# A windowed-attention stack: the local attention output transposed in 32x32 blocks by VectorE, in place of TensorE transposes and ScalarE copies

## The chip, the cores and the metric

The kernel runs on one core of a Trainium2 chip. The metric is the device time of one execution in microseconds; here the median of 3 runs. The core has TensorE (PE, matmuls, writes PSUM only), VectorE (DVE), ScalarE (ACT), GpSimd (POOL) and SyncE (SP, which issues the DMAs). Each engine works through its own queue of instructions in order and is synchronised with the others by semaphores.

## The reference

Input is x of 8 x 512 x 128 (f32). With xn = layer norm of x, the output is x + global_attention(xn) + local_stack(xn). The local stack has 6 layers. Each layer, with `shift` moving the second half of the channels down by one token:

```
x = attn_layer(shift(x)) + x ;  x = ffn_layer(shift(x)) + x
attn_layer: q, k, v = split(x @ Wqkv) in 16 heads of 64; q, k l2-normalised, scaled, rotated
            windows of 32 tokens; each window attends to itself and the window before it, masked
            out = softmax(q k^T * 8) v, per head;   return out (tokens x 1024) @ Wo
ffn_layer:  layer norm, W1 (a and gate), a * gelu(gate), W2
```

The change concerns the step between softmax(...) v and the product with Wo: `out` has tokens in partitions where it is computed, and Wo's product needs channels in partitions.

## The kernel before

Layer norm and the global attention come first (the first 690 us or so). Then `windowed_stack` runs 48 units, one for each layer and batch element (512 tokens, four tiles of 128). xT holds x with channels in partitions.

A unit is cut into stages, named by a kind and a tile number: `q0` (projection), `square_q0`, `rotate_q0`, `norms0`, `root0`, `scale_q0` (normalising and rotating), `qT0`, `kT0` (PE transposes), `s0` (scores, DVE subtracts the maximum), `exp0`, `r0` (transposes of the probabilities), `va0`, `vb0` (probabilities times v, heads 0-7 and 8-15), `o0` (transposes of the output), `wo`, `mean`, `var`, `z`, `h0` to `h2`, `y` (feed-forward).

The order of the stages on each engine is written out by hand in PE_ORDER, DVE_ORDER, ACT_ORDER, POOL_ORDER and SP_ORDER. A name with `-` belongs to the previous unit, so two units overlap. Nothing is planned at run time: an engine takes the stages in that order, and each stage waits for its inputs (`x_filled`, `x_read`, events such as `rooted`). PSUM is four slots of two banks; SLOTS_OF names the stages that share a slot, and a stage on PE also waits until the stage before it in its slot has been read.

Around the change, for each tile:
- PE `va`, `vb` (`products`): 32x32 blocks of probabilities times v. One column of v is 1, so that column 64 of each 65 is the sum. Window order in PSUM is that of WINDOWS = (1, 3, 0, 2).
- DVE `va`, `vb` (L836, L837): reciprocal of the sums, product into `o` (tokens in partitions, 1024 elements), a link semaphore between the two.
- PE `o` (L967 with `ident,o`): eight 128x128 transposes into PSUM. ACT `o` (L926): one copy into `oT` [128, 8, 512], windows put back in order. It waits for the previous unit's `wo`.
- PE `wo` (L1037): eight matmuls of 512 columns over the chunks of oT, after the copy of tile 3. DVE `residual` adds x into x1; ACT `shift` (L938, L872, L873) makes xs2 from it; PE `mean`, DVE `center` (L846) and so on.

At a layer's end SP waits for DVE's `y` and loads the feed-forward weights, w_o among them, in five DMAs (`load_ff`); PE, DVE and ACT wait for all five. w_qkv is loaded in three parts as their last use passes. POOL does `add` (cosq + sinq, L734) and the steps of the square root (L726). The v halves are shifted by a window into `vb` with DMAs.

Of the kernel before, what the change touches and what calls it, by code (L numbers as in the profile page):

```python
# [12 lines left out]
P = 128  # L13
D = 128
# [17 lines left out]
NJ = 3  # L32
# [167 lines left out]
def global_attention(nc, io, res, xT, ident):  # L200
# [6 lines left out]
    with ExitStack() as ctx:  # L207
# [227 lines left out]
        def _(pe):  # L435
# [75 lines left out]
PE_ORDER = stages(  # L511
    "o0- r1- s2- q0 kT3- va1- k0 vb1- qT3- r2- o1- s3- va2- vb2- q1 r3- k1 o2- qT0 va3- vb3- kT0 k2 o3- s0 wo- q2 "
    "v0 mean- qT1 r0 var- v1 kT1 k3 va0 s1 h0- h1- h2- vb0 q3 v2 qT2 y- kT2 v3 ")
DVE_ORDER = stages(
# [3 lines left out]
ACT_ORDER = stages(  # L518
    "o0- r1- v3- square_q0 kT3- square_k0 exp2- qT3- r2- o1- exp3- square_q1 r3- o2- qT0 square_k1 kT0 o3- "
    "square_k2 exp0 shift- square_q2 v0 square- qT1 r0 root- kT1 v1 gate0- square_k3 gate1- gate2- exp1 square_q3 "  # L520
# [12 lines left out]


FILLS = {"q": (TPB, "dve"), "k": (TPB, "dve"), "v": (TPB, "act"), "qT": (TPB, "act"), "kT": (TPB, "act"),
         "s": (TPB, "dve"), "r": (TPB, "act"), "va": (TPB, "dve"), "vb": (TPB, "dve"), "o": (TPB, "act"),
         "wo": (1, "dve"), "mean": (1, "dve"), "var": (1, "act"), "h": (NJ, "dve"), "y": (1, "dve")}
# [3 lines left out]
          "q_scaled": ("dve", TPB), "k_scaled": ("dve", TPB), "probs": ("act", TPB),  # L541
          "xs2_ready": ("act", 1), "centered_sq": ("act", 1), "z_ready": ("dve", 1), "gates": ("act", NJ)}
EVENTS.update({kind + "_filled": ("pe", n) for kind, (n, _) in FILLS.items()})
# [4 lines left out]
VTILES = 3  # L548
WINDOWS = (1, 3, 0, 2)


def windowed_stack(nc, io, xT, ident):
# [5 lines left out]
    with ExitStack() as ctx:  # L558
# [37 lines left out]
        o = sb("o", [P, 2, 4, 2, DH])  # L596
        oT = sb("oT", [P, QCH, SEQ])
        x1 = sb("x1", [P, SEQ])
# [21 lines left out]
        def wait_tile(eng, name, unit, t, back=1):  # L620

            wait(eng, name, unit + (t - back) // TPB, (t - back) % TPB)
# [39 lines left out]
        def _(sp):  # L662
# [4 lines left out]
            def load_ff(l):  # L667
                sp.dma_start(w_o[:, :, :], io["w_o"][l].rearrange("(c p) n -> p c n", p=P)).then_inc(S["w_ff"], 16)
                sp.dma_start(w_1[:, :, :, :].rearrange("p a j n -> p (a j n)"), io["w_1"][l]).then_inc(S["w_ff"], 16)
                sp.dma_start(w_2[:, :, :], io["w_2"][l].rearrange("(j p) n -> p j n", p=JW)).then_inc(S["w_ff"], 16)  # L670
                sp.dma_start(b_1[:, :, :].rearrange("p a j -> p (a j)"), io["b_1"][l]).then_inc(S["w_ff"], 16)
                sp.dma_start(vec[:, :], io["vec"][l]).then_inc(S["w_ff"], 16)
# [66 lines left out]
        def _(dve):  # L739
# [49 lines left out]
            def stage(kind, n, unit, batch, before, starts):  # L789
# [40 lines left out]
                elif kind in ("va", "vb"):  # L830
                    a = ("va", "vb").index(kind)
                    wait(dve, kind + "_filled", unit, n)

                    wait_tile(dve, "o_filled", unit, n)
                    ps = slot(kind, n)[:, :, 0:4 * VA].rearrange("p r (w d) -> p r w d", d=VA)
                    link(nc.vector.reciprocal(rden[:, a], ps[:, :, :, DH]), kind, 0)  # L836
                    nc.vector.tensor_tensor(o[:, a].rearrange("p w r d -> p r w d"), ps[:, :, :, 0:DH],  # L837
                                            rden[:, a, :, :, None].broadcast_to([P, 2, 4, DH]), ALU.mult).then_inc(S[kind + "_read"], 1)
                elif kind == "residual":
                    wait(dve, "wo_filled", unit)  # L840
# [25 lines left out]
        def _(act):  # L866
# [12 lines left out]
            def stage(kind, n, unit, batch, before, starts):  # L879
# [7 lines left out]
                elif kind == "v":  # L887

                    old, unit_of = (0, unit) if n == VTILES else ((TPB - 1 if n == 0 else n), unit - 1)
                    wait(act, "vb_filled", unit_of, old)  # L890
                    wait_vb(act, unit_of, old)
# [25 lines left out]
                elif kind == "r":  # L917
                    wait(act, "r_filled", unit, n)

                    wait_tile(act, "vb_filled", unit, n)  # L920
                    nc.scalar.copy(probT[:, :, :], flat("r", n).rearrange("p (c n) -> p c n", n=P)).then_inc(S["r_read"], 1)
                elif kind == "o":
                    wait(act, "o_filled", unit, n)

                    wait(act, "wo_filled", unit - 1)
                    nc.scalar.copy(oT[:, :, n * P:(n + 1) * P].rearrange("p c (w n) -> p w c n", n=WIN),  # L926
                                   flat("o", n).rearrange("p (w c n) -> p w c n", w=4, n=WIN)).then_inc(S["o_read"], 1)
                elif kind == "next":
# [27 lines left out]
        def _(pe):  # L956
# [6 lines left out]

            def transposes(kind, n, src, place=lambda c: c):
                for c in range(8):
                    k = place(c)
                    last = nc.tensor.transpose(flat(kind, n)[:, k * P:(k + 1) * P], src[:, c * P:(c + 1) * P], ident[:, :])  # L967
                return last
# [17 lines left out]
            def products(kind, t):  # L986
                a = ("va", "vb").index(kind)
                for r in range(2):
                    for n, v in enumerate((va, vb)):
                        for g in range(4):  # L990

                            last = nc.tensor.matmul(  # L992
                                slot(kind, t)[32 * g:32 * g + 32, r, 2 * n * VA:2 * (n + 1) * VA],
                                probT[:, 4 * a + 2 * r + n, 32 * g:32 * g + 32],
                                v[:, t % VTILES, :, 2 * (4 * a + g) + r, :],
                                start=True, stop=True, skip_group_check=True)
                return last

            def stage(kind, n, unit, batch, before, starts):
# [22 lines left out]
                elif kind in ("va", "vb"):  # L1022
                    if kind == "va":
                        wait(pe, "r_read", unit, n)
                        wait_vb(pe, unit, n)
                    passed(pe)
                    last = products(kind, n)
                elif kind == "o":
                    wait(pe, "va_read", unit, n)
                    wait(pe, "vb_read", unit, n)  # L1030

                    last = transposes(kind, n, o[:, :, :, :, :].rearrange("p a w r d -> p (a w r d)"),
                                      lambda c: 2 * WINDOWS[c % 4] + c // 4)
                elif kind == "wo":
                    wait(pe, "o_read", unit, TPB - 1)
                    for c in range(QCH):
                        last = nc.tensor.matmul(slot("wo")[:, 0, :], w_o[:, c, :], oT[:, c, :], start=c == 0, stop=c == QCH - 1)  # L1037
                elif kind == "mean":
# [126 lines left out]
```

## Time and profile before

| | before |
|---|---|
| median of 3 runs (lowest, highest) | 4495.01 us (4487.22, 4496.09) |
| span of the profiled execution | 4494.6 us (no other time of it is given) |
| PE busy | 4032.1 us, 90% |
| DVE busy | 3861.7 us, 86% |
| ACT busy | 2887.1 us, 64% |
| POOL busy | 1723.6 us, 38% |
| DMA, q1 | 122.47 MB, 11.4% of 16 engines |
| granted TensorE clock, mean of the span | 0.976 of full speed |

Busy time counts an engine's instructions, not register, branch, semaphore or DMA-issuing ones. Matmuls are pipelined, so a group's duration overlaps with the next group's, and the step from one start to the next is what a group costs. DVE instructions overlap slightly too. An idle time in front of an instruction is put down to what released it. PEld is PE's loading of weights, which runs beside the matmuls.

### The profile page before, as it was taken

To read this page: it belongs to the slowest core of one execution; us is meant where nothing else is said; L and a number is where in the kernel's file an instruction comes from. 1 tells how busy PE (TensorE), PEld (TensorE's weight loads), DVE (VectorE), ACT (ScalarE), POOL (GpSimd) and SP (SyncE) were. 2 spreads that over 40 slices of the span, in tenths; PEclk is the share of its full clock that TensorE was granted. 3 is DMA by queue.
4 is the path that set the end of the run, shared out by engine and by line. 5 is a ranking of instruction groups with operands and counts; after the bars stand their busy time and mean duration, and the time that the engine had idled before them with its cause. 6 is when DMAs were issued, how large, how long until landed. Compare 5 with 4: busy or idle time off the path is not lost. (4 is left out here: it accounts for less than half of the span.)

```text
span 4494.6 us, 104653 instructions
## 1 busy us (share of the span) xinstructions
PE 4032.1 (90%) x38560; PEld 2304.6 (51%) x38560; DVE 3861.7 (86%) x5604; ACT 2887.1 (64%) x3434; POOL 1723.6 (38%) x3226
## 2 busy tenths in 40 slices
PE   5888885999998999989999989999899999899996
PEld 2333333555555555555555555555455555555554
DVE  6888877898988999978999879898889998798985
ACT  3666663676766666666767666666666666576764
POOL 2222213444443434434444434444343434344441
PEclk8999997999999999999999999999999999999998
DMA  0000002010111111120101111110211111110102
GB/s 25 1 1 1 1 1 71 22 32 21 32 33 37 27 26 27 26 53 19 34 19 31 38 36 27 23 30 21 52 23 29 24 26 43 32 32 19 35 18 56
DMA packets 65070, 123.99 MB, mean 28 GB/s; under 512 B 15684, under 2 KB 37576, under 8 KB 64968
## 3 DMA queue, kind: packets, MB, share of 16 engines
q1 hardware_dynamic: 64968, 122.47, 11.4%
q8 instruction: 84, 1.38, 0.1%
q14 instruction: 18, 0.15, 0.0%
HBM read 21.99 MB, written 4.19 MB: 6 GB/s over the span
## 5 line engine op out<-in xcount | busy, mean ns | idle before, releaser
L734 POOL TENSOR_TENSOR cosq<-cosq,sinq 128x1024 f32<-128x1024 f32 x384 | 970.9, 2528 | 1665.5 <-DVE sinq L784 1665.5
L1010 PE MATMUL slot<-w_qkv,xs 128*128 128x512 f32 x2304 | 1096.5, 606 | 54.3 <-ACT xs L873 26.6
L819 DVE TENSOR_TENSOR qk<-cosq,ry 128x1024 f32<-128x1024 f32 x384 | 587.7, 1550 | 93.2 <-POOL ry L726 48.3
L1010 PEld LDWEIGHTS slot<-w_qkv,xs 128*128 128x128 f32 x2304 | 406.4, 191 | 474.4 <-issue 379.7
L784 DVE TENSOR_TENSOR sinq<-slot,table 128x512 f32<-128x512 f32 x768 | 490.6, 680 | 0.0
L781 DVE TENSOR_TENSOR cosq<-slot,table 128x1024 f32<-128x1024 f32 x384 | 467.9, 1218 | 18.8 <-ACT sq L885 6.8
L910 ACT COPY kT<-slot 64x1024 f32<-64x1024 f32 x384 | 386.6, 1007 | 120.6 <-PE slot L967 116.8
L916 ACT ACTIVATE prob<-prob 128x1024 f32<-128x1024 f32 x192 | 203.0, 1057 | 388.8 <-DVE prob L828 387.1
L803 DVE TENSOR_REDUCE ss<-sq 128x32 f32<-128x2048 f32 x192 | 437.3, 2277 | 11.3 <-ACT sq L885 11.3
L967 PEld LDWEIGHTS slot<-ident,qk 128*128 128x128 f32 x3072 | 345.1, 142 | 180.1 <-issue 92.8
L885 ACT ACTIVATE sq<-slot 128x1024 f32<-128x1024 f32 x384 | 392.5, 1022 | 66.9 <-PE slot L1010 65.6
L967 PE MATMUL slot<-ident,qk 128*128 128x128 f32 x3072 | 409.8, 277 | 16.1 <-DVE o L837 7.9
L979 PE MATMUL slot<-kT,qT 128*32 128x128 f32 x12288 | 417.2, 276 | 7.5 <-issue 7.5
L979 PEld LDWEIGHTS slot<-kT,qT 128*32 128x32 f32 x12288 | 313.0, 110 | 106.6 <-issue 106.4
L372 DVE TENSOR_REDUCE at_rowmax<-at_slot 128x1 f32<-128x512 f32 x512 | 317.1, 684 | 50.6 <-PE at_slot L459 50.3
L1037 PE MATMUL slot<-oT,w_o 128*128 128x512 f32 x768 | 342.4, 599 | 1.2 <-ACT oT L926 1.2
L992 PE MATMUL slot<-va,probT 128*32 128x130 f32 x6144 | 318.0, 277 | 22.9 <-DVE sinq L784 22.9
L425 ACT ACTIVATE at_probs<-at_slot 128x1024 f32<-128x1024 f32 x256 | 245.8, 1027 | 130.2 <-PE at_slot L473 130.1
L1047 PE MATMUL slot<-xs,w 128*114 128x512 f32 x576 | 261.0, 603 | 70.3 <-DVE xs L854 70.3
L992 PE MATMUL slot<-vb,probT 128*32 128x130 f32 x6144 | 312.7, 273 | 0.0
L827 DVE TENSOR_REDUCE smax<-slot 128x16 f32<-128x1024 f32 x192 | 233.5, 1216 | 67.1 <-PE slot L979 67.1
L726 POOL TENSOR_TENSOR rt<-ry 128x32 f32<-128x32 f32 x576 | 137.3, 238 | 377.1 <-DVE ry L810 346.9
(130 smaller groups left out, 6568.9 us busy)
## 6 DMA issues: line engine op xcount, KB each, us to landing
vb<-va SPq DMA_DIRECT2D x720, 130.0 KB, 2.3
w_qkv<-in_w_qkv SPq DMA_DIRECT2D x18, 512.0 KB, 4.5
w_o<-in_w_o SPq DMA_DIRECT2D x6, 512.0 KB
w<-in_w SPq DMA_DIRECT2D x6, 342.0 KB
res<-in_x SPq DMA_DIRECT2D x4, 512.0 KB, 6.2
kept<-res SPq DMA_DIRECT2D x1, 2048.0 KB, 8.7
out<-fin_res SPq DMA_DIRECT2D x8, 256.0 KB, 2.4
w<-in_w SPq DMA_DIRECT2D x6, 171.0 KB
```

The costliest lines, as they stand in the source:

```text
L734: nc.gpsimd.tensor_tensor(cosq[:, side], cosq[:, side], sinq[:, side], ALU.add).then_inc(S["qk"[side] + "_added"], 1)
L781: nc.vector.tensor_tensor(cosq[:, side].rearrange("p h a d -> p h (a d)"), ps.rearrange("p h a d -> p h (a d)"), cos[:, None, :].broadcast ...
L784: last = nc.vector.tensor_tensor(sinq[:, side, :, half, :], ps[:, :, 1 - half, :], sin[:, None, half * H:half * H + H].broadcast_to([P, HE ...
L803: nc.vector.reduce_sum(ss[:, :], sq[:, :, :, :].rearrange("p a h d -> p (a h) d"), AX.X).then_inc(S["sumsq"], 1)
L819: nc.vector.tensor_tensor(qk[:, side], cosq[:, side].rearrange("p h a d -> p h (a d)"), ry[:, side * HEADS:(side + 1) * HEADS, None].broad ...
L885: nc.scalar.activation(sq[:, "qk".index(name)].rearrange("p h d -> p (h d)"), flat(name, n), ACT.Square).then_inc(S[name + "_squared"], 1)
L910: nc.scalar.copy(own[rows, :, r, WIN:WIN + P], ps[rows])
L967: last = nc.tensor.transpose(flat(kind, n)[:, k * P:(k + 1) * P], src[:, c * P:(c + 1) * P], ident[:, :])
L979: last = nc.tensor.matmul(slot("s", t)[32 * g:32 * g + 32, a, :].rearrange("p (r k) -> p r k", r=2)[:, :, n * DH:(n + 1) * DH], qT[:, c, t ...
L992: last = nc.tensor.matmul(slot(kind, t)[32 * g:32 * g + 32, r, 2 * n * VA:2 * (n + 1) * VA], probT[:, 4 * a + 2 * r + n, 32 * g:32 * g + 3 ...
L1010: last = nc.tensor.matmul(slot(kind, n)[:, i, :], xs[:, n * P:(n + 1) * P], w_qkv[:, "qkv".index(kind), i * SEQ:(i + 1) * SEQ], start=True ...
L1037: last = nc.tensor.matmul(slot("wo")[:, 0, :], w_o[:, c, :], oT[:, c, :], start=c == 0, stop=c == QCH - 1)
```

## The change

The `o` stages leave PE and ACT. DVE gets a stage `turn` per tile, behind `vb`: one transpose instruction that turns every 32x32 block of `o` (128x1024) into `oT`. It doesn't move blocks across partitions, so a partition of oT holds the 32 channels of one half of a head in one of four groups of heads; w_o's rows are reordered on the host to match, which makes its load one contiguous row per partition. `products` writes the windows in natural order at a pitch of 66. `wo` reads its 512 columns in runs of 32.

```diff
 PE_ORDER = stages(
-    "o0- r1- s2- q0 kT3- va1- k0 vb1- qT3- r2- o1- s3- va2- vb2- q1 r3- k1 o2- qT0 va3- vb3- kT0 k2 o3- s0 wo- q2 "
+    "r1- s2- q0 kT3- va1- k0 vb1- qT3- r2- s3- va2- vb2- q1 r3- k1 qT0 va3- vb3- kT0 k2 s0 wo- q2 "
     "v0 mean- qT1 r0 var- v1 kT1 k3 va0 s1 h0- h1- h2- vb0 q3 v2 qT2 y- kT2 v3 ")
 DVE_ORDER = stages(
-    "scale_k3- scale_q3- s2- rotate_q0 va1- vb1- norms0 rotate_k0 s3- va2- vb2- scale_q0 rotate_q1 scale_k0 va3- "
-    "vb3- norms1 rotate_k1 s0 scale_q1 scale_k1 rotate_k2 residual- center- rotate_q2 norms2 z- va0 s1 scale_q2 hid0- "
-    "scale_k2 hid1- vb0 hid2- rotate_k3 norms3 rotate_q3 y- ")
+    "scale_k3- scale_q3- s2- rotate_q0 va1- vb1- turn1- norms0 rotate_k0 s3- va2- vb2- turn2- scale_q0 rotate_q1 scale_k0 va3- "
+    "vb3- turn3- norms1 rotate_k1 s0 scale_q1 scale_k1 rotate_k2 residual- center- rotate_q2 norms2 z- va0 s1 scale_q2 hid0- "
+    "scale_k2 hid1- vb0 turn0 hid2- rotate_k3 norms3 rotate_q3 y- ")
 ACT_ORDER = stages(
-    "o0- r1- v3- square_q0 kT3- square_k0 exp2- qT3- r2- o1- exp3- square_q1 r3- o2- qT0 square_k1 kT0 o3- "
+    "r1- v3- square_q0 kT3- square_k0 exp2- qT3- r2- exp3- square_q1 r3- qT0 square_k1 kT0 "
     "square_k2 exp0 shift- square_q2 v0 square- qT1 r0 root- kT1 v1 gate0- square_k3 gate1- gate2- exp1 square_q3 "
...
     "k0 kT0 s0 q1 kT1 s1 q2 qT2 kT2 s2 va3 h2",
-    "va0 o0 va1 o1 va2 o2 q3 vb3 o3 wo mean var h1",
+    "va0 va1 va2 q3 vb3 wo mean var h1",
     "q0 v0 r0 k1 r1 vb1 r2 vb2 k3 y",)
...
 FILLS = {"q": (TPB, "dve"), "k": (TPB, "dve"), "v": (TPB, "act"), "qT": (TPB, "act"), "kT": (TPB, "act"),
-         "s": (TPB, "dve"), "r": (TPB, "act"), "va": (TPB, "dve"), "vb": (TPB, "dve"), "o": (TPB, "act"),
+         "s": (TPB, "dve"), "r": (TPB, "act"), "va": (TPB, "dve"), "vb": (TPB, "dve"),
          "wo": (1, "dve"), "mean": (1, "dve"), "var": (1, "act"), "h": (NJ, "dve"), "y": (1, "dve")}
...
           "q_scaled": ("dve", TPB), "k_scaled": ("dve", TPB), "probs": ("act", TPB),
-          "xs2_ready": ("act", 1), "centered_sq": ("act", 1), "z_ready": ("dve", 1), "gates": ("act", NJ)}
+          "xs2_ready": ("act", 1), "centered_sq": ("act", 1), "z_ready": ("dve", 1), "gates": ("act", NJ),
+          "turned": ("dve", TPB)}
 EVENTS.update({kind + "_filled": ("pe", n) for kind, (n, _) in FILLS.items()})
...
 WINDOWS = (1, 3, 0, 2)
+PITCH = VA + 1
...
         o = sb("o", [P, 2, 4, 2, DH])
-        oT = sb("oT", [P, QCH, SEQ])
+        oT = sb("oT", [P, TPB, 2, 4, 2, 2, 32])
         x1 = sb("x1", [P, SEQ])
...
             def load_ff(l):
-                sp.dma_start(w_o[:, :, :], io["w_o"][l].rearrange("(c p) n -> p c n", p=P)).then_inc(S["w_ff"], 16)
+                sp.dma_start(w_o[:, :, :].rearrange("p c n -> p (c n)"), io["w_o"][l]).then_inc(S["w_ff"], 16)
                 sp.dma_start(w_1[:, :, :, :].rearrange("p a j n -> p (a j n)"), io["w_1"][l]).then_inc(S["w_ff"], 16)
...
-                    wait_tile(dve, "o_filled", unit, n)
-                    ps = slot(kind, n)[:, :, 0:4 * VA].rearrange("p r (w d) -> p r w d", d=VA)
+                    wait_tile(dve, "turned", unit, n)
+                    ps = slot(kind, n)[:, :, 0:4 * PITCH].rearrange("p r (w d) -> p r w d", d=PITCH)
                     link(nc.vector.reciprocal(rden[:, a], ps[:, :, :, DH]), kind, 0)
...
                                             rden[:, a, :, :, None].broadcast_to([P, 2, 4, DH]), ALU.mult).then_inc(S[kind + "_read"], 1)
+                elif kind == "turn":
+
+                    wait(dve, "vb_read", unit, n)
+                    wait(dve, "wo_filled", unit - 1)
+                    nc.vector.transpose(oT[:, n, :, :, :, :, :].rearrange("p a w r e t -> p (a w r e t)"),
+                                        o[:, :, :, :, :].rearrange("p a w r d -> p (a w r d)")).then_inc(S["turned"], 1)
                 elif kind == "residual":
...
                     old, unit_of = (0, unit) if n == VTILES else ((TPB - 1 if n == 0 else n), unit - 1)
-                    wait(act, "vb_filled", unit_of, old)
+                    for name in ("va", "vb"):
+                        wait(act, name + "_filled", unit_of, old)
                     wait_vb(act, unit_of, old)
...
-                    wait_tile(act, "vb_filled", unit, n)
+                    for name in ("va", "vb"):
+                        wait_tile(act, name + "_filled", unit, n)
                     nc.scalar.copy(probT[:, :, :], flat("r", n).rearrange("p (c n) -> p c n", n=P)).then_inc(S["r_read"], 1)
-                elif kind == "o":
-                    wait(act, "o_filled", unit, n)
-
-                    wait(act, "wo_filled", unit - 1)
-                    nc.scalar.copy(oT[:, :, n * P:(n + 1) * P].rearrange("p c (w n) -> p w c n", n=WIN),
-                                   flat("o", n).rearrange("p (w c n) -> p w c n", w=4, n=WIN)).then_inc(S["o_read"], 1)
                 elif kind == "next":
...
-            def transposes(kind, n, src, place=lambda c: c):
+            def transposes(kind, n, src):
                 for c in range(8):
-                    k = place(c)
-                    last = nc.tensor.transpose(flat(kind, n)[:, k * P:(k + 1) * P], src[:, c * P:(c + 1) * P], ident[:, :])
+                    last = nc.tensor.transpose(flat(kind, n)[:, c * P:(c + 1) * P], src[:, c * P:(c + 1) * P], ident[:, :])
                 return last
...
                             last = nc.tensor.matmul(
-                                slot(kind, t)[32 * g:32 * g + 32, r, 2 * n * VA:2 * (n + 1) * VA],
+                                slot(kind, t)[32 * g:32 * g + 32, r, 0:4 * PITCH].rearrange("p (w d) -> p w d", d=PITCH)[
+                                    :, (1 - n)::2, 0:VA],
                                 probT[:, 4 * a + 2 * r + n, 32 * g:32 * g + 32],
...
                 elif kind in ("va", "vb"):
-                    if kind == "va":
-                        wait(pe, "r_read", unit, n)
-                        wait_vb(pe, unit, n)
+                    wait(pe, "r_read", unit, n)
+                    wait_vb(pe, unit, n)
                     passed(pe)
                     last = products(kind, n)
-                elif kind == "o":
-                    wait(pe, "va_read", unit, n)
-                    wait(pe, "vb_read", unit, n)
-
-                    last = transposes(kind, n, o[:, :, :, :, :].rearrange("p a w r d -> p (a w r d)"),
-                                      lambda c: 2 * WINDOWS[c % 4] + c // 4)
                 elif kind == "wo":
-                    wait(pe, "o_read", unit, TPB - 1)
+                    wait(pe, "turned", unit, TPB - 1)
                     for c in range(QCH):
-                        last = nc.tensor.matmul(slot("wo")[:, 0, :], w_o[:, c, :], oT[:, c, :], start=c == 0, stop=c == QCH - 1)
+                        a, r, half = c // 4, c // 2 % 2, c % 2
+                        last = nc.tensor.matmul(slot("wo")[:, 0, :], w_o[:, c, :], oT[:, :, a, :, r, half, :],
+                                                start=c == 0, stop=c == QCH - 1)
                 elif kind == "mean":
...
         "qk_scale": np.broadcast_to(scales, (DEPTH, P, 2 * DH)),
-        "w_o": f["ffn_Wo"],
+        "w_o": f["ffn_Wo"].reshape(DEPTH, 2, 4, 4, 32, D).transpose(0, 2, 4, 1, 3, 5).reshape(DEPTH, P, QCH * D),
         "w_1": w1.reshape(DEPTH, D, 2 * NJ * JW),
```

## Rows read from the trace of the kernel before

**Rows 1.** The page, part 1: busy time and share of the span of each engine.
```profile
PE 4032.1 (90%) x38560; PEld 2304.6 (51%) x38560; DVE 3861.7 (86%) x5604; ACT 2887.1 (64%) x3434; POOL 1723.6 (38%) x3226
```

**Rows 2.** ACT's instruction at L938, by tile: count, shortest/median/longest ns, first and last start.
```profile
L938 ACT ACTIVATE xs<-zero x48: 199/199/201, 810.3 to 4448.0; 64x1 f32<-64x1 f32 x48
```

**Rows 3.** Stretches: length, then busy us (count) of PE, PEld, DVE, ACT, POOL; clock; DMA.
```profile
2677.66:2753.68 76.02, 72.04 (x735) 43.06 (x734) 69.00 (x85) 51.47 (x62) 32.02 (x56) 1.00 0.12 27
2591.05:2677.66 86.61, 74.35 (x735) 45.05 (x734) 67.19 (x85) 51.45 (x62) 31.99 (x56) 0.94 0.15 36
```

**Rows 4.** DVE's waits, 2677.66 to 2753.68 us: total, times, longest us.
```profile
DVE xc L846 <- PE slot L1040: 2.8, 1, 2.8
DVE qk L819 <- POOL ry L726: 1.1, 1, 1.1
DVE rden L836 <- PE slot L992: 0.8, 2, 0.5
DVE smax L827 <- PE slot L979: 0.5, 1, 0.5
DVE sqc L850 <- ACT sqc L945: 0.3, 1, 0.3
DVE ss L803 <- ACT sq L885: 0.2, 1, 0.2
```

**Rows 5.** DVE and POOL in order of time: start, duration us, instruction, [idle before it].
```profile
2711.43 4.35 DVE L819 TENSOR_TENSOR qk<-cosq,ry 128x1024 f32<-128x1024 f32 x2 [1.13 <-POOL ry L726]
...
2721.80 0.21 DVE L836 RECIPROCAL rden<-slot 128x8 f32<-128x8 f32 x1 [0.46 <-PE slot L992]
...
2722.04 0.69 DVE L837 TENSOR_TENSOR o<-slot,rden 128x512 f32<-128x512 f32 x1
...
2722.65 2.27 DVE L803 TENSOR_REDUCE ss<-sq 128x32 f32<-128x2048 f32 x1
...
2745.85 2.36 POOL L734 TENSOR_TENSOR cosq<-cosq,sinq 128x1024 f32<-128x1024 f32 x1
...
2747.24 3.19 DVE L819 TENSOR_TENSOR qk<-cosq,ry 128x1024 f32<-128x1024 f32 x2
```

**Rows 6.** PE in order of time, same unit.
```profile
2709.91 1.04 PE L967 MATMUL slot<-ident,o 128*128 128x128 f32 x8
...
2710.79 1.04 PE L967 MATMUL slot<-ident,prob 128*128 128x128 f32 x8
...
2712.98 0.39 PE L972 MATMUL slot<-mask,ident 128*128 128x512 bf16 x1
...
2720.65 0.43 PE L992 MATMUL slot<-va,probT 128*32 128x130 f32 x8 [0.43 <-DVE sinq L784]
...
2731.61 1.06 PE L967 MATMUL slot<-ident,prob 128*128 128x128 f32 x8 [0.60 <-ACT prob L916]
```

**Rows 7.** DVE instructions by line: count, shortest/median/longest ns.
```profile
L388 DVE STREAM_TRANSPOSE at_oT<-at_po x32: 716/717/718, 84.9 to 673.5; 128x512 f32<-128x512 f32 x32
L803 DVE TENSOR_REDUCE ss<-sq x192: 2272/2275/2287, 710.6 to 4406.2; 128x32 f32<-128x2048 f32 x192
L819 DVE TENSOR_TENSOR qk<-cosq,ry x384: 1209/1215/3319, 717.6 to 4416.5; 128x1024 f32<-128x1024 f32 x192
```

**Rows 8.** In order of time: a weight change (DVE and PE), and the trace's end.
```profile
2551.17 1.22 DVE L827 TENSOR_REDUCE smax<-slot 128x16 f32<-128x1024 f32 x1 [2.97 <-PE slot L979]
...
2632.15 1.94 PE L967 MATMUL slot<-ident,o 128*128 128x128 f32 x8 [8.69 <-DMA vec<-in_vec]
...
2633.89 1.92 PE L967 MATMUL slot<-ident,prob 128*128 128x128 f32 x8
...
2637.57 0.39 PE L972 MATMUL slot<-mask,ident 128*128 128x512 bf16 x1
...
2639.13 1.22 DVE L827 TENSOR_REDUCE smax<-slot 128x16 f32<-128x1024 f32 x1 [4.74 <-PE slot L979]
...
4449.61 2.05 PE L1040 MATMUL slot<-xs,ones 128*128 128x512 f32 x2 [2.36 <-ACT xs L873]
```

## The prediction

> **What bounds the kernel now.** I read the page's totals first. TensorE (PE) is busy for 90% of the span and VectorE (DVE) for 86% [rows 1], so either could be the limit. The work repeats, so the next view is one steady repetition. A program in the windowed stack handles 48 units (6 layers x 8 batch elements); ACT's small write at L938 occurs once per unit. It has 48 starts, 810.3 to 4448.0 us [rows 2]: 47 intervals, of which the last has no next unit behind it. I reckon with the 46 others. A middle interval takes 76.02 us, and in it PE is busy 72.04 and DVE 69.00 us [rows 3]. The longer interval in the same group is one where the weights change.
>
> Busy time doesn't say who waits for whom. DVE's own waits in that interval add up to 2.8+1.1+0.8+0.5+0.3+0.2 = 5.7 us [rows 4], so 70.3 of its 76.0 us is occupied. The question is which of these waits could absorb new DVE work. I followed each in the timeline:
> - 2.8 us (xc at L846): DVE writes x1, ACT shifts it, PE averages it, DVE goes on. No other DVE work stands between the two in DVE's order. It can't shrink because DVE gets busier.
> - 1.1 us (qk at L819, stages `scale_k3-`): DVE has seeded the square root, Pool (POOL) does 12 small steps, DVE fills the time with `rotate_q3` and `y-`. It starts from DVE's seeds, so it moves with DVE.
> - 0.8 us (rden) is two waits. The 0.46 before `vb1-` [rows 5]: PE had itself waited 0.43 for DVE's sinq [rows 6], because the PSUM slot of `vb1` holds `q0`. It hangs on DVE. The other 0.39, before `va3-`, ends with PE products that follow a long PE run. It is real slack.
> - 0.5 us (smax, `s0`) ends with PE scores.
> - 0.3 us (sqc) is at the end of an ACT run that begins with DVE's x1; 0.2 us (ss, `norms3`) ends with ACT's square. Only the last is slack for work put just ahead of it.
>
> So the loop that sets 76 us already runs mainly through DVE, and most of DVE's idle time is the latency of loops that DVE itself starts. PE's 4 us of idle time are mostly waits for them.
>
> **What the change removes.** Per unit, 4 groups of 8 PE transposes (`o`), each with one ACT copy of 128x1024 into oT. A group's duration is 1.04 us but the next group starts 0.88 us after it [rows 6], so PE is relieved of 4 x 0.88 = 3.5 us and ACT of four copies. Almost nothing of this is on the loop above. PE waits longer instead. Where it does reach the end is at the weight changes (below).
>
> **What it adds.** Per unit, 4 DVE transposes of 128x1024 f32, SBUF to SBUF, each behind a wait for the multiply just before it. The trace has no such instruction, but it has the same operation on 512 elements from PSUM: 716/717/718 ns [rows 7]. For the other 512 elements I use the slope between the shortest L819 (1209 ns, 1024 elements) and L803 (2275 ns, 2048 elements): 1.04 ns each, 533 ns. That gives 1.25 us. Bounds: 0.72 us if it handles two elements at a time, and 3.3 us, the longest L819, if it were held up each time by POOL [rows 7]. L803, which like the new instruction has one SBUF input, is within 2272 and 2287 ns in all 192 cases while L819 with two spreads from 1209 to 3319. I therefore take 1.25.
>
> Around it: without a wait the next DVE instruction starts 0.61 us after a 0.69 us multiply starts, and with one 0.03 us after the previous end (0.24 against 0.21) [rows 5]. The new wait therefore costs 0.69+0.03-0.61 = 0.11 us, and the following instruction recovers 0.08. One `turn` is 0.11+1.25-0.08 = 1.28 us, four are 5.12 us.
>
> The Trainium skill (VectorE: DVE Perf Modes, The three transpose paths) lists 390 ns for a TensorE transpose of 128x128 bf16 against 311 ns on VectorE. By this the exchange of 32 such tiles would look like a gain, 12.5 us of TensorE for 10.0 of VectorE per unit (an estimate from that page). The rows differ on both sides: a TensorE one costs the stream 0.11 us here, and the f32 DVE row makes eight tiles 1.25 us.
>
> **Where each turn falls.**
> - `turn0`, between `vb0` and `hid2`: all gates' inputs but the last were released earlier, so ACT's path is unchanged. `norms3` had 0.20 us of waiting. DVE is late by 1.28-0.20 = 1.08 us, and so are the seeds, POOL's root and `scale_k3-`. PE's `y-` waits for `hid2`, but comes over 1 us behind it.
> - `turn1`, before `norms0`: 1.28 in full. Behind it on DVE stand norms0, rotate_k0 and s3; ACT's exponential, then PE's `r3-`, wait for s3.
> - `turn2`, before `scale_q0`: 1.28, less the 0.39 of `va3-`, since PE comes there earlier by the missing `o2`. `qT0` on PE waits some 0.3 us for scale_q0, which leaves va3 still in time.
> - `turn3`, before `norms1`: 1.28 in full. The 0.5 us at `s0` vanish but win nothing: `scale_q1`, `scale_k1` take 3.19 us instead of 2.3 because POOL's cosq addition runs until 2748.21 [rows 5], and that addition follows norms1 through POOL. This wait is only renamed.
> - The mean on PE comes 0.1 us earlier, as PE is now idle before it.
>
> Sum: 5.12-0.20-0.39-0.10 = 4.43 us per interval, 76.0 becomes 80.4. DVE would be busy 69.0+5.0 = 74.0 us of it, PE 72.0-3.5 = 68.5.
>
> **Weight changes.** Each of 5 stretches over two intervals. In the first DVE waits 2.97 us for PE's scores behind a stall of PE's issue; there the 1.08 us of turn0 is absorbed, and the missing `o0` (0.88) brings the scores forward: -1.96. In the second, everything stands until the feed-forward weights are there, then PE does o0, r1, s2 while DVE waits 4.74 us; o0's step is 1.74 us there, at the lower clock: -1.74 [rows 8]. Together -3.7 each, -18.5 in all. The w_o load in 4 KB rows instead of 512 B may bring up to 2 us per change; it is one of five loads awaited together, so I take 0.
>
> **Costed at nothing.** The products write rows at a pitch of 66 and windows in another order: same columns, same DVE reads (bounds +-0.1 us per unit). wo's input is read in runs of 32: PE has about 1 us to spare before the mean. The extra `va_filled` waits on ACT concern earlier PE work. Ahead of the first and behind the last of the 46 intervals, turns partly fall into waits and the o3-copy latency before the last wo goes: 0, +-5 us.
>
> Forecast: 4494.6 + 46 x 4.43 - 18.5 = 4679.9, say 4680 us. The page gives the profiled execution's span, 4494.6, and no other time of it; the median of the timed runs is 4495.0, so I add nothing.
>
> **Rivals.**
> 1. *Faster: the idle time on DVE absorbs the turns.* If every wait in rows 4 could shrink, the interval would be DVE's occupied time, 70.3+5.1 = 75.4, -0.6 us: 4494.6-28-18.5 = 4448 us. It decides if PE, 90% busy, is the true bound and DVE's waits are all its doing. For: PE's higher busy share. Against: PE's recorded waits end with DVE or with ACT work that DVE released, and 2.8+1.1 us come from chains that DVE starts. Break-even needs 4.4 us more slack than I found. 7%.
> 2. *The transposes run at twice the rate* (0.72 us, lower bound): a turn costs 0.75, the interval +3.00-0.69 = +2.3: 4494.6+106-17 = 4584 us. Against: the 512-element row has the plain rate, if from PSUM. 8%. The Trainium skill (Vector Engine (DVE) Microarchitecture Reference, Performance modes) names copy, cast, tensor_scalar and tensor_tensor as what has faster modes enabled, and the transpose isn't among them; no run shows it yet for SBUF.
> 3. *The PE clock falls.* PE's idle gaps grow: before `vb1` 0.43+0.88+1.08 = 2.4 us, before `r3` 0.60+0.88+1.28 = 2.8 us [rows 6]. At the end of the trace PE takes 2.05 us for the mean's two matmuls after a gap of 2.36 us [rows 8], which is slow for 512 columns: the same engine does eight of 128 in 1.04 [rows 6]. From the two levels at a weight change: o0, r1 and half of s2 took 5.4 us at 1.2 GHz, then 2.4 [rows 8], against 3.1 in mid-layer [rows 6], +2.3. Once per unit and unhidden: 46 x 2.3 = +106, 4786 us; half hidden about 4735. Against: those gaps stand alone between dense stretches, and the steady interval grants 1.00 [rows 3]. 12%.
> 4. *Nothing to be told* (within 0.2%, about what this kernel's measurement can resolve, 9 us): some mix of 1 and 2. 3%.
>
> **Chances.** My forecast 70%, its own range 4650 to 4710 (turn 1.2 to 1.4 us, loads, pitch). Rivals 7, 8, 12 and 3%. Slower by over 0.2%: 0.90; within: 0.03; faster: 0.07. The 8-in-10 range, reaching toward rivals 2 and 3: 4600 to 4740.
>
> **What would show it.** A mid-layer interval of 80.4 us; DVE STREAM_TRANSPOSE at 1.25 us x192; xc's wait still 2.7 to 2.8 and the POOL wait still 1.1; rden's waits near 0.46 and smax's near 0 in an interval; PE waiting over 2 us at `vb1` and `r3`; granted clock still 1.00; DVE's wait at a weight change 1.7 us shorter. I am wrong if DVE's waits in an interval sum to under 2 us (rival 1), if the transposes take 0.7 us, or if the clock of a mid-layer interval is under 0.95.

## The result and the profile after

The changed kernel takes 4684.4 us (median of 4 runs, 4681.55 to 4686.1), the kernel before in the same series 4495.6 (median of 4): a ratio of 1.042, 95% interval 1.0405 to 1.0435. It is slower by 189 us. The forecast was 4680. The profiled execution took 4685.08 us with a span of 4683.3.

Part 1 of the page of the changed kernel, against [rows 1]:

```profile
PE 3833.7 (82%) x36769; PEld 2136.3 (46%) x37024; DVE 4114.1 (88%) x5796; ACT 2708.4 (58%) x3242; POOL 1722.9 (37%) x3226
```

PE lost 198 us of busy time and gave all of it back as idle time. DVE gained 252 us, more than the kernel became longer. These totals alone don't say which engine sets the time: they would fit any case in which one engine gets heavier and another lighter.

The instruction that starts a unit's feed-forward part, now at L942, by tile, and one mid-layer interval and one at a weight change (columns as in [rows 3]: length, busy us of PE, PEld, DVE, ACT and POOL, granted clock, DMA):

```profile
L942 ACT ACTIVATE xs<-zero x48: 199/199/200, 809.5 to 4638.5; 64x1 f32<-64x1 f32 x48
```

```profile
2775.37:2855.84 80.47, 68.33 (x699) 39.66 (x702) 74.30 (x89) 47.74 (x57) 32.01 (x56) 1.00 0.11 25
2685.28:2775.37 90.09, 70.38 (x699) 41.23 (x702) 72.50 (x89) 47.68 (x57) 31.98 (x56) 0.94 0.14 35
```

A mid-layer interval takes 80.47 us where it took 76.02 [rows 3]; the 35 others in mid-layer lie between 80.46 and 80.52. PE is busy for 68.3 us of it instead of 72.0, DVE for 74.3 instead of 69.0, and the clock is granted in full, as before.

DVE's waits in that interval (total, times, longest us), to be laid beside [rows 4]:

```profile
DVE xc L854 <- PE slot L1039: 2.8, 1, 2.8
DVE qk L821 <- POOL ry L728: 1.1, 1, 1.1
DVE rden L838 <- PE slot L995: 0.6, 2, 0.5
DVE sqc L858 <- ACT sqc L949: 0.3, 1, 0.3
```

This is the core of the case. Of 5.7 us of waiting, 0.9 went (0.5 smax, 0.2 ss, 0.2 of rden) and 4.8 stayed as they were, although 5 us of work had been put on the engine that waits. The largest two are still 2.8 and 1.1.

The new transposes, with the two lines that the cost had been worked out from (compare [rows 7]; ns shortest/median/longest):

```profile
L845 DVE STREAM_TRANSPOSE oT<-o x192: 1245/1245/1246, 752.5 to 4627.6; 128x1024 f32<-128x1024 f32 x192
L821 DVE TENSOR_TENSOR qk<-cosq,ry x384: 1180/1212/3311, 714.0 to 4606.9; 128x1024 f32<-128x1024 f32 x192
L805 DVE TENSOR_REDUCE ss<-sq x192: 2242/2268/2285, 707.0 to 4596.6; 128x32 f32<-128x2048 f32 x192
```

All 192 take 1245 or 1246 ns; forecast 1250. DVE around `turn1` and the pair of scales behind `turn3`, then POOL's addition before that pair:

```profile
2820.44 0.21 DVE L838 RECIPROCAL rden<-slot 128x8 f32<-128x8 f32 x1 [0.46 <-PE slot L995]
...
2820.68 0.69 DVE L839 TENSOR_TENSOR o<-slot,rden 128x512 f32<-128x512 f32 x1
...
2821.41 1.25 DVE L845 STREAM_TRANSPOSE oT<-o 128x1024 f32<-128x1024 f32 x1
...
2822.57 2.24 DVE L805 TENSOR_REDUCE ss<-sq 128x32 f32<-128x2048 f32 x1
...
2848.77 3.83 DVE L821 TENSOR_TENSOR qk<-cosq,ry 128x1024 f32<-128x1024 f32 x2
```

```profile
2848.02 2.36 POOL L736 TENSOR_TENSOR cosq<-cosq,sinq 128x1024 f32<-128x1024 f32 x1
```

Without a turn the next instruction followed the multiply's start by 0.61 us [rows 5]; now norms0 follows by 2822.57-2820.68 = 1.89, so the turn costs 1.28, of which the reduction behind it gives 0.03 back (2.24 us instead of 2.27). In the last DVE row the two scales take 3.83 us instead of 3.19 [rows 5]: DVE comes 0.64 us earlier relative to POOL's addition, which runs to 2850.38, and has to stand there instead. That is the wait for PE's scores at `s0` under another name.

The wait before `va3-` shrank and didn't vanish, first in the kernel before, then in the changed one:

```profile
2737.22 0.21 DVE L836 RECIPROCAL rden<-slot 128x8 f32<-128x8 f32 x1 [0.39 <-PE slot L992]
```

```profile
2838.14 0.21 DVE L838 RECIPROCAL rden<-slot 128x8 f32<-128x8 f32 x1 [0.17 <-PE slot L995]
```

PE in the same interval, against [rows 6]:

```profile
2776.97 1.10 PE L1039 MATMUL slot<-xs,ones 128*128 128x512 f32 x2 [1.25 <-ACT xs L881]
...
2819.29 0.43 PE L995 MATMUL slot<-va,probT 128*32 128x130 f32 x8 [0.43 <-DVE sinq L786]
...
2827.93 1.98 PE L1014 MATMUL slot<-w_qkv,xs 128*128 128x512 f32 x4 [0.88 <-DVE sinq L786]
...
2831.50 1.06 PE L970 MATMUL slot<-ident,prob 128*128 128x128 f32 x8 [1.58 <-ACT prob L925]
...
2836.99 0.43 PE L995 MATMUL slot<-va,probT 128*32 128x130 f32 x8 [1.46 <-DVE sinq L786]
```

PE now waits for DVE in more places. Its longest gap is 1.6 us, before `r3`, where I had expected 2.8: part of the delay falls before `q1` (0.88) instead, which waits for the PSUM slot that DVE's rotate_k0 still reads. Before `vb1` it is still 0.43 and not 2.4: PE had lost the time before that. The granted clock of the interval stayed at full speed. A longer gap does stand before `vb1` in the first stretch of each weight change of the changed kernel, 2.01 to 2.26 us; here is one, with its whole stretch:

```profile
2648.73 0.43 PE L995 MATMUL slot<-va,probT 128*32 128x130 f32 x8 [2.26 <-DVE sinq L786]
```

```profile
2602.93:2685.28 82.35, 68.29 (x699) 39.65 (x702) 75.87 (x95) 47.74 (x57) 32.00 (x56) 1.00 0.17 45
```

The clock of that stretch is 1.00 too, and so it is in the first stretch of the four other changes of this kernel.

Finally a weight change: PE of the changed kernel, one more row of PE before (its first half of the scores, which belongs to [rows 8]), and DVE of the changed kernel (`s2-` in the first stretch and in the second):

```profile
2727.08 1.96 PE L970 MATMUL slot<-ident,prob 128*128 128x128 f32 x8 [8.71 <-DMA vec<-in_vec]
...
2729.40 1.94 PE L982 MATMUL slot<-kT,qT 128*32 128x128 f32 x32 [0.36 <-issue]
...
2731.27 0.61 PE L975 MATMUL slot<-mask,ident 128*128 128x512 bf16 x1
```

```profile
2636.16 1.48 PE L979 MATMUL slot<-kT,qT 128*32 128x128 f32 x32
```

```profile
2641.90 1.21 DVE L829 TENSOR_REDUCE smax<-slot 128x16 f32<-128x1024 f32 x1
...
2733.32 1.22 DVE L829 TENSOR_REDUCE smax<-slot 128x16 f32<-128x1024 f32 x1 [3.85 <-PE slot L982]
```

### The profile page after: what moved, and what is told of

Same layout as the page of the kernel before. It is cut to its first block and busy times, and to the rows that moved or that the text cites. A ratio compares the mean times of both kernels' runs of the same rounds, so it can differ in the third digit from the quotient of the medians.

```text
span 4683.3 us, 101413 instructions
## 1 busy us (share of the span) xinstructions
PE 3833.7 (82%) x36769; PEld 2136.3 (46%) x37024; DVE 4114.1 (88%) x5796; ACT 2708.4 (58%) x3242; POOL 1722.9 (37%) x3226
## 5 line engine op out<-in xcount | busy, mean ns | idle before, releaser
L821 DVE TENSOR_TENSOR qk<-cosq,ry 128x1024 f32<-128x1024 f32 x384 | 615.9, 1623 | 92.5 <-POOL ry L728 48.2
L970 PE MATMUL slot<-ident,prob 128*128 128x128 f32 x1536 | 213.2, 283 | 191.7 <-ACT prob L925 78.0
```

Source lines behind the costliest of these rows:

```text
L821: nc.vector.tensor_tensor(qk[:, side], cosq[:, side].rearrange("p h a d -> p h (a d)"), ry[:, side * HEADS:(side + 1) * HEADS, None].broad ...
L970: last = nc.tensor.transpose(flat(kind, n)[:, c * P:(c + 1) * P], src[:, c * P:(c + 1) * P], ident[:, :])
```

## The experiments

Each was timed in rounds with the kernel before on the same chip. "Interval" is the usual distance of two unit starts in the mid-layer. The two weight stretches are given as what they exceed the interval by, added over the five changes; both columns come from one profiled execution of each kernel. What lies outside the 46 intervals took 912 to 931 us in these executions, with no pattern that follows the edits, so a difference of some us between two times says less than one between two intervals.

| kernel | time, us | ratio to before (95%) | interval, us | first, second stretch, us |
|---|---|---|---|---|
| before | 4493.6 to 4495.6 by series | 1 | 76.02 | 20.9, 51.5 |
| changed | 4684.4 | 1.042 (1.0405-1.0435) | 80.48 | 9.3, 48.3 |
| e1 add turns only | 4698.3 | 1.0448 (1.0425-1.047) | 80.57 | 15.2, 52.9 |
| e2 tiny turns | 4502.0 | 1.0018 (1.0005-1.0032) | 76.8 | 10.0, 46.2 |
| e3 side edits only | 4496.8 | 1.0001 (0.9987-1.0014) | 76.04 | 23.3, 51.3 |
| e4 turn0 late | 4644.3 | 1.0326 (1.0302-1.0349) | 79.58 | 13.6, 49.3 |
| e5 turn3 late | 4624.3 | 1.0282 (1.0265-1.0299) | 79.32 | 9.4, 46.1 |
| e6 both late | 4581.9 | 1.0196 (1.0178-1.0214) | 78.38 | 11.6, 48.2 |
| e7 before, affine on ACT | 4415.5 | 0.983 (0.981-0.9851) | 74.40 | 21.4, 54.1 |
| e8 changed, both late, affine on ACT | 4507.0 | 1.0029 (1.0017-1.004) | 76.74 | 9.9, 44.7 |

**e1: the turns without the relief.** The kernel before, with the turn stages in DVE_ORDER where the change has them; the `o` stages of PE and ACT stay.

```diff
+        spare = sb("spare", [P, 4 * 2 * 2 * DH])
...
+                elif kind == "turn":
+                    wait(dve, "vb_read", unit, n)
+                    wait_tile(dve, "turned", unit, n)
+                    nc.vector.transpose(spare[:, :], o[:, :, :, :, :].rearrange("p a w r d -> p (a w r d)")).then_inc(S["turned"], 1)
```

> The kernel before, with the four DVE transposes of 128x1024 per unit added and nothing taken away: they write a spare buffer that nothing reads, PE's o transposes and ACT's o copies stay. Theory (DVE sets the mid-layer interval, PE's and ACT's relief is worth nothing there): the interval rises from 76.02 to 80.4 us, as with the whole change; at the weight changes only the first stretch absorbs 1.1 us; time 4495 + 46 x 4.43 - 5 = 4694 us, within 4680 to 4705. Rival (the removed PE work did pay, and without its removal the turns cost more): up to 3.5 us per interval more, 4700 to 4850 us. Second rival (the cost is in the edits around the turns): under 4600 us.

Measured: 4698.3 us. The stretch of one mid-layer interval and DVE's waits in it:

```profile
2869.14:2949.70 80.56, 72.50 (x735) 43.24 (x734) 74.39 (x89) 51.41 (x61) 32.09 (x56) 1.00 0.11 25
```

```profile
DVE xc L852 <- PE slot L1046: 2.9, 1, 2.9
DVE qk L821 <- POOL ry L728: 1.1, 1, 1.1
DVE rden L838 <- PE slot L998: 0.6, 2, 0.5
DVE sqc L856 <- ACT sqc L951: 0.3, 1, 0.3
```

PE does its full 72.5 us of work again, and the interval is 80.56. The transposes and copies that the change removed, 3.7 us of PE and 3.7 us of ACT per interval, are therefore worth 0.09 us in mid-layer. DVE's waits are those of the changed kernel to a tenth. This decides against the rival in which PE's relief pays. What the relief does bring is at the weight changes: the changed kernel's two columns are together 10.5 us lower, and the times differ by 13.9.

**e2: the relief without the turns.** oT is cleared once at the start and then only written by the small blocks.

```diff
-                    nc.vector.transpose(oT[:, n, :, :, :, :, :].rearrange("p a w r e t -> p (a w r e t)"),
-                                        o[:, :, :, :, :].rearrange("p a w r d -> p (a w r d)")).then_inc(S["turned"], 1)
+                    nc.vector.transpose(oT[:, n, 0, 0, 0, 0, :], o[:, 0, 0, 0, 0:32]).then_inc(S["turned"], 1)
```

> The changed kernel with each transpose cut to one 128x32 block, waits and order kept; the rest of oT stays at zero, so most of the attention output is left out. Theory: a turn costs 0.11+0.2 = 0.3 us, 1.2 in all, of which 0.2 and 0.39 fall into waits; the interval is 76.5 us although PE is 3.5 us lighter; time 4495 + 46 x 0.5 - 15 = 4503 us, within 4480 to 4520. Rival (PE's relief is worth its 3.5 us once DVE is not loaded): interval 73.5 to 74, 4370 to 4400 us.

Measured: 4502.0 us. A mid-layer interval, and the small transpose:

```profile
2832.88:2909.70 76.82, 68.97 (x703) 39.63 (x703) 70.33 (x89) 47.76 (x58) 32.20 (x56) 1.00 0.11 26
```

```profile
L846 DVE STREAM_TRANSPOSE oT<-o x192: 211/211/213, 748.6 to 4447.0; 128x32 f32<-128x32 f32 x192
```

PE is busy for 69.0 us, near the 68.3 of the changed kernel, and the interval is 0.8 us longer than before, not shorter. With e1 this closes both sides: take PE's work away, with 0.2 us turns in place of 1.25 us ones, and nothing is won; put DVE's work on alone and everything is lost. The interval was forecast at 76.5. The 0.3 us that it lies above that are 13 us in all, and the time met its forecast because what lies outside the intervals took 12 us less than before in its profile, which I can't explain: that was luck.

**e3: pitch, order of windows, layout of oT and w_o.** The kernel before, with PITCH, `products`, `wo` and w_o as in the change, and ACT's copy into the new layout:

```diff
-                    nc.scalar.copy(oT[:, :, n * P:(n + 1) * P].rearrange("p c (w n) -> p w c n", n=WIN),
-                                   flat("o", n).rearrange("p (w c n) -> p w c n", w=4, n=WIN)).then_inc(S["o_read"], 1)
+                    nc.scalar.copy(oT[:, n, :, :, :, :, :].rearrange("p a w r e t -> p (a w r e t)"),
+                                   flat("o", n)).then_inc(S["o_read"], 1)
```

> The kernel before with the side edits alone: product rows at a pitch of 66, windows in natural order, oT written and read in runs of 32 in the new layout, w_o loaded as one row per partition. PE transposes and ACT copies stay, so the blocks reach wo in a wrong place: this changes what is computed. Theory: costed at nothing; interval 76.0 +-0.1, each weight change up to 2 us shorter, 4485 to 4500 us. Rival (reading in short runs or the pitch slows PE or DVE): interval above 76.3, over 4510 us.

Measured: 4496.8 us, ratio 1.0001; interval 76.04. The side edits are free. The larger rows of w_o's load bring nothing at a weight change either (51.3 against 51.5); the up to 2 us that I had allowed for them came from no row.

**e4: turn0 in front of the wait for POOL.**

```diff
-    "scale_k2 hid1- vb0 turn0 hid2- rotate_k3 norms3 rotate_q3 y- ")
+    "scale_k2 hid1- vb0 hid2- rotate_k3 norms3 rotate_q3 y- turn0 ")
```

> The changed kernel with turn0 moved behind y- on DVE, just ahead of the 1.14 us in which DVE waits for POOL's root. Theory: the step of 1.2 us falls into that wait, the 1.08 us that turn0 cost in its old place come back; interval 79.4, time 4684 - 50 = 4634 us, within 4625 to 4645. Rival (a DVE transpose costs its 1.28 us wherever it stands, because something else than DVE's order is behind it, as contention): no gain, 4675 to 4690 us.

Measured: 4644.3 us, interval 79.58. DVE in its new place (and norms3 before it):

```profile
2858.90 2.29 DVE L805 TENSOR_REDUCE ss<-sq 128x32 f32<-128x2048 f32 x1 [0.20 <-ACT sq L893]
...
2864.17 0.74 DVE L869 SCALAR_TENSOR_TENSOR xT<-slot,vec,x 128x512 f32 x1
...
2864.82 1.23 DVE L845 STREAM_TRANSPOSE oT<-o 128x1024 f32<-128x1024 f32 x1
...
2866.04 4.36 DVE L821 TENSOR_TENSOR qk<-cosq,ry 128x1024 f32<-128x1024 f32 x2
```

The transpose stands where DVE waited 1.14 us, and the wait is gone from the row of qk at 2866.04. In return the 0.20 in front of ss is back. This unit starts at 2832.24, so qk comes 33.80 us into it; in the kernel before, which has no turn there, it was 2711.43-2677.66 = 33.77 [rows 3, rows 5]. In this place the turn costs 0.03 us at most. In its old place it cost 0.93: the reciprocal of `vb1-`, the next wait for PE, comes 2721.80-2677.66 = 44.14 us into the unit before the change and 2820.44-2775.37 = 45.07 in the changed kernel. So the same instruction costs 0.93 in one place and next to nothing in the other, and the 0.90 between them is what e4 won. The forecast of 79.4 was too low because it took 1.08 for the price in the old place. With longer weight stretches (13.6 and 49.3 us, against 9.3 and 48.3 in the changed kernel; three of the first ones hold a spell at half clock, of which more at e6) the time is 10 us above the forecast, at the upper end of its range.

**e5, e6: turn3 behind norms1, alone and with turn0 late.**

```diff
-    "vb3- turn3- norms1 rotate_k1 s0 scale_q1 scale_k1 rotate_k2 residual- center- rotate_q2 norms2 z- va0 s1 scale_q2 hid0- "
+    "vb3- norms1 turn3- rotate_k1 s0 scale_q1 scale_k1 rotate_k2 residual- center- rotate_q2 norms2 z- va0 s1 scale_q2 hid0- "
```

> The changed kernel with turn3 moved behind norms1 (before rotate_k1). The seeds of norms1 then come 1.28 us earlier, and POOL's root1 and add_k1, which hold scale_q1 and scale_k1 up (3.83 us for the two in the changed kernel, 2.3 without POOL), follow the seeds, not the turn. Theory: the turn falls into POOL's latency; PE's wo, q2 and v0 then come close to the mean and take 0.3 us back: interval 80.47 - 1.0 = 79.5, time 4684 - 46 = 4638 us, within 4620 to 4650. Rival (the loop runs through DVE's own work only, not through POOL): no gain, 4680 to 4690.

> The changed kernel with turn0 behind y- (79.57 us an interval when alone) and turn3 behind norms1. Theory: the two gains stand in different waits and add: interval 78.6, 4684 - 86 = 4598 us, within 4585 to 4615. Even so slower than the kernel before, since turn1 and turn2 have no wait near them. Rival (both hide in the same slack): no better than the better one alone, 4635.

Measured: 4624.3 us with an interval of 79.32, and 4581.9 with 78.38. DVE in e5: the turn, and the pair of scales that took 3.83:

```profile
2977.45 1.24 DVE L845 STREAM_TRANSPOSE oT<-o 128x1024 f32<-128x1024 f32 x1
...
2983.30 2.72 DVE L821 TENSOR_TENSOR qk<-cosq,ry 128x1024 f32<-128x1024 f32 x2
```

The pair takes 2.72 us now. The seeds of norms1 went ahead of the turn, so POOL's chain ends earlier relative to DVE, and 1.16 of the 1.28 us came back. The 0.3 that I had charged for PE's mean didn't fall due: DVE's xc starts 2.73 us into the unit in e5 as in the changed kernel. So e5 gained more than forecast. Both moves together give 0.90+1.16 = 2.06, measured 80.48-78.38 = 2.10: different waits, and they add. The time of e6 is 3 us below its range (4585 to 4615), since its interval is 0.2 us under the forecast of 78.6, which is 10 us in all, and what lies outside the intervals took 9 us less than in the changed kernel. The two other turns stayed where they were.

e6 also has, in the first stretch of its second weight change, what I had priced as the clock rival: PE stands for 2.04 us, and the four matmuls behind the gap take 3.17 us instead of 1.98.

```profile
1953.14 3.17 PE L1014 MATMUL slot<-w_qkv,xs 128*128 128x512 f32 x4 [2.04 <-issue]
```

```profile
1913.66:1995.88 82.22, 69.71 (x699) 40.30 (x702) 74.78 (x95) 47.79 (x57) 32.10 (x56) 0.98 0.17 45
```

The granted clock was half from 1953.74 to 1957.15 us, and this stretch is 82.22 us long where the first stretches of the four other changes take 80.24 to 80.40.

**e7, e8: DVE made lighter elsewhere.** The new ACT stage `affine-` stands between `v1` and `gate0-`; e8 has the orders of e6 too.

```diff
-                    nc.vector.tensor_scalar(z[:, :], z[:, :], vec[:, 0:1], vec[:, 1:2], ALU.mult, ALU.add).then_inc(S["z_ready"], 1)
...
+                elif kind == "affine":
+                    act.wait_ge(S["ff_link"], 2 * unit + 2)
+                    nc.scalar.activation(z[:, :], z[:, :], ACT.Identity, scale=vec[:, 0:1], bias=vec[:, 1:2]).then_inc(S["z_ready"], 1)
```

> Not the change: the kernel before, PE transposes and ACT copies of o kept, with the last step of z (multiply by ln_g, add ln_b: DVE L854, 2.46 us, of which 1.9 us is waiting for POOL) done by ACT as one activation. Theory (what DVE is relieved of shortens the loop until PE's scores and vb0 products are late): DVE wins 2.4 us, 1.0 is lost again to waits for PE at s1 and vb0; interval 74.6, 4495 - 65 = 4430 us, within 4400 to 4460. Rival (PE, 90% busy, is the bound, and DVE's load matters only when added): under 0.5 us per interval, 4470 to 4495.

> The changed kernel with both turns late and z's last step on ACT. Theory: the gains add, 78.6 - 1.4 = 77.2 us an interval, 4530 us, within 4500 to 4560, still slower than e7 by about 100 us: lighter PE and ACT do not pay as long as DVE is the last in the loop. Rival (with DVE lighter, PE is the bound, so that the o work it no longer has pays here): 4400 to 4440, as fast as e7 or faster.

Measured: 4415.5 us, faster than before by 1.7%, and 4507.0. In e7 a mid-layer interval, DVE's waits and the new ACT instruction:

```profile
2854.00:2928.40 74.40, 71.01 (x731) 43.04 (x734) 66.65 (x84) 52.35 (x63) 32.02 (x56) 1.00 0.12 27
```

```profile
DVE xc L846 <- PE slot L1041: 2.9, 1, 2.9
DVE rden L836 <- PE slot L993: 1.3, 3, 0.5
DVE qk L819 <- POOL ry L726: 1.1, 1, 1.1
DVE smax L827 <- PE slot L980: 1.0, 2, 0.5
```

```profile
2867.69 0.82 ACT L946 ACTIVATE xs<-xs,vec 128x512 f32<-128x512 f32 x1
```

DVE is relieved of a step of 2.5 us. About 1.1 of it turns into two waits for PE (smax 0.5 to 1.0, rden 0.8 to 1.3), and the 0.2 us before ss are gone in return, so that 76.02-74.40 = 1.62 shorten the interval. In e8 the same edit brings 78.38-76.74 = 1.64: no more than on the kernel with PE's full load, and the same two waits for PE appear, 0.5 us each. So even with this off DVE, taking the `o` transposes from PE is not what the kernel lacks, and e7 with the old transposes stays 2% ahead of e8 (4415.5 against 4507.0). e7 is the fastest kernel of this study, and the turn is no part of it.

## Why the prediction was right, and where its terms were off

- *What bounds the kernel.* Right. The reasoning went by which waits could shrink, not by which engine is busiest. 2.8, 1.1, 0.46 and 0.3 us were named as not absorbable, and all four are there after the change and in e1.
- *The transpose and its step.* 1.25 and 1.28 us; measured 1.245 and 1.28.
- *Slack.* The sum came out, its parts less so. Counted from the start of the unit, DVE is 0.93 us later than before from norms3 on because of `turn0`, `turn1` adds 1.25, `turn2` 1.02 and `turn3` 1.26, 4.46 in all. I had 1.08, 1.28, 0.89 and 1.28, less 0.10 for an earlier mean. At `turn0` 0.29 was absorbed and not 0.20: once ss no longer waits, it also starts 0.08 us before the end of the sinq ahead of it. Of the 0.39 before `va3-`, 0.17 stayed: `va3` on PE had to wait 1.46 us for DVE's sinq, the last of the PE rows, since its PSUM slot holds `q1` until rotate_q1 has read it. I had not seen that wait. The mean's 0.10 didn't come: PE starts it 1.60 us into the unit in both kernels. These errors cancel to 0.03, which is luck.
- *smax is only renamed.* Right, and e5 shows the chain through POOL behind it.
- *Weight changes.* The most mis-sized term: -18.5 us forecast, -14.8 measured (first stretches 20.9 to 9.3, second 51.5 to 48.3), and again two errors of opposite sign. I had taken one change for all five.
  - First stretch: 1.96 us each forecast, 2.3 measured. The whole of the 2.97 us vanished [rows 8], DVE's row at 2641.90 shows none; at the five changes that wait was 0.82, 2.10, 2.97, 2.44 and 2.73 us before, and it is gone at all five. PE's stall of issue is gone with it. Why it stood there is open: e1, which has all of PE's instructions, keeps a wait of 2.50 and 2.26 us at two changes and has none at three.
  - Second stretch: 1.74 us each forecast, 0.64 measured. DVE's wait fell by 4.74-3.85 = 0.89 us in the change shown; at the five it was 4.57, 3.87, 4.74, 3.80 and 4.70 before and is 3.90, 3.77, 3.85, 3.73 and 3.76 now. I had priced o0 at the 1.2 GHz at which it ran. But PE did not spend less time at that clock. After it had begun again it ran at half clock for another 4.6 to 4.9 us at three changes of the kernel before and for 2.9 and 3.1 at the two others, where the wait hardly fell; in the changed kernel this is 5.1 to 5.4 us at all five. Other work ran slowly in place of o0: the first half of the scores took 1.94 us where it had taken 1.48. Why the low clock reached further isn't shown. It isn't the missing work alone: e2 lacks o0 too and has 2.9 to 6.1 us.
- *The sum.* 46 x 4.46 = 205.2, weight changes -14.8, both ends -1.8: 188.6, against 188.7 between the spans. Forecast 203.8-18.5 = 185.3.
- *Rivals.* DVE's idle time absorbing the turns: refuted by the waits after the change. Transposes at twice the rate: refuted by 1245 ns. The Trainium skill (Vector Engine (DVE) Microarchitecture Reference, Performance modes) leaves this operation out of those with faster modes, and by that rule the trace agrees. PE's clock falling: the clock of mid-layer intervals stayed at 1.00. It was priced on gaps of 2.4 and 2.8 us that did not come about there. The nearest are in the first weight stretches. The changed kernel's gaps of 2.01 to 2.26 us there left the clock at 1.00 five times, but a gap of 2.24 in the kernel before (it ends at 1311.44 us) was followed by a fall to half clock at 1312.67, and e6 has the same behind 2.04. So what the rival describes does happen in these runs behind gaps of this size, though not each time; it did not happen in mid-layer, where no gap of the changed kernel is over 1.6 us.

## What to carry to other kernels

Before moving work between engines, sort the receiving engine's idle time by what releases it: a wait that hangs on a chain which the same engine started moves along with the added work and absorbs nothing, and here that was 2.8+1.1+0.46+0.3 = 4.7 of 5.7 us on an engine that was only 86% busy. Moving work off the busiest engine (PE, 90%) was worth 0.09 us of an interval of 80.57. If an instruction must be added, its place decides its price: 1.23 us of work cost 0.93 us in front of the seeds of a chain through POOL and 0.03 at most behind them, in the wait for that chain. And a price read from one of five places that look alike (here the weight changes) can be the exception: look at all five.

## What the runs showed of the hardware beyond what was expected

- VectorE's block transpose of f32 takes 211 ns for 32 elements per partition (e2), 1245 for 1024 from SBUF, and 717 for 512 from PSUM [rows 7]: about 178 ns plus 1.04 ns per element. The 192 of the changed kernel lie within 1 ns of each other, though in 94 of them one of POOL's 128x1024 additions ran at the same time.
- The DVE instruction with two per-partition scalars at L854 takes 2.46 us (median of 48) beside POOL's addition, and 0.55 us in the one case, at the end, that has none beside it. ACT does the same in 0.82 us (e7).
- PE gaps of the same size left the clock alone or were followed by a fall: 2.01 to 2.26 us left it at 1.00 five times in the changed kernel, while after 2.24 us in the kernel before and after 2.04 in e6 it fell to half for a while. What tells the cases apart isn't shown.
- After PE's standstill of 8 to 10 us at a weight change it ran at half clock for another 2.9 to 6.1 us of work. Both ends of that range are from the same kernel (e2).
